# Layer 0 of a two-layer scan network: next steps projected into the sums' banks, fewer states weighed by GpSimd, output projection between the next image's spreads

## The reference, cut to what matters

```python
x_dbl = einsum('bkdl,kcd->bkcl', xs, x_proj_weight)      # per order k: 12 step columns, 16 B, 16 C
dts = einsum('bkrl,kdr->bkdl', dts, dt_projs_weight)     # the step projection
delta = softplus(dts + dt_projs_bias)                    # the steps
h = exp(delta * A) * h + (delta * u) * B                 # the scan, for each state n
y = sum over n of (h * C_n)                              # weighing, and the sum over states
```

## Time and profile before

| | |
|---|---|
| time, median of 3 | 15351.56 us (15350.93 to 15354.0) |
| profiled execution, its own time | 15355.73 us |
| its span, first to last instruction | 15353.9 us |
| mean granted TensorE clock | 0.898 of full speed |

### The profile page before, as it was taken

One profiled execution on the slowest core, in us unless ns is written; L12 is line 12 of the kernel. 1 busy time (PEld: TensorE's weight loads), 2 busy tenths in 40 slices (PEclk: granted clock), 3 DMA queues, 4 the chain that ended last, 5 costly groups with the idle time before them and its releaser, 6 DMA issues.

```text
span 15353.9 us, 137291 instructions
## 1 busy us (share of the span) xinstructions
PE 11962.6 (78%) x45056; PEld 6538.9 (43%) x45056; DVE 13974.8 (91%) x8019; ACT 10343.2 (67%) x14003; POOL 13679.9 (89%) x5828
## 2 busy tenths in 40 slices
PE   6777877778777787777877778777787777877778
PEld 4543345433444334443345433444334443345433
DVE  8998989989899899998999989999898998989988
ACT  5666766667666676666766667666676666766667
POOL 7997989979899798997889978899789997899978
PEclk8898988989889898898988989889898898988989
DMA  5662256622566225662256622666226662266622
GB/s 188 213 214 95 88 188 215 213 93 85 193 214 215 90 82 196 215 215 86 82 201 213 216 85 80 204 215 214 84 77 209 215 214 81 77 212 214 213 76 76
DMA packets 687758, 2440.08 MB, mean 159 GB/s; under 512 B 78268, under 2 KB 100040, under 8 KB 687048
## 3 DMA queue, kind: packets, MB, share of 16 engines
q1 hardware_dynamic: 687048, 2431.29, 46.6%
HBM read 2415.26 MB, written 15.73 MB: 158 GB/s over the span
## 4 chain that ended last, share of the span: by engine, by line
POOL 48%; issue 18%; DMA 11%; DVE 10%; PE 10%; ACT 3%; POOLq 0%; DVEq 0%; SPq 0%; ACTq 0%
POOL room L1186 26%; DMA room<-bc_rows 11%; POOL room L1229 7%; POOL room L1195 4%; POOL room L1232 4%; POOL room L1221 4%; DVE room L1420 4%; PE bank L720 3%; POOL room L1176 2%; PE bank L454 2%; DVE room L1355 2%; DVE u L1312 1%; DVE room L1440 1%; DVE room L1429 1%; PE bank L792 1%
## 5 line engine op out<-in xcount | busy, mean ns | idle before, releaser
L1355 DVE TENSOR_TENSOR_SCAN room<-bank,room 128x1024 f32<-128x1024 f32 x3072 | 6903.6, 2275 | 327.5 <-issue 170.2
L1186 POOL TENSOR_TENSOR room<-room 128x1024 f32<-128x1024 f32 x3072 | 7168.0, 2374 | 0.6
L930 ACT ACTIVATE bank<-room,a 128x1024 f32<-128x1024 f32 x3072 | 3429.7, 1127 | 1046.0 <-DVE room L1355 1031.7
L720 PE MATMUL bank<-room,identity 128*128 128x512 f32 x6144 | 3007.4, 640 | 855.5 <-DVE room L1440 733.2
L1420 DVE TENSOR_TENSOR_SCAN room<-bank,room 128x1024 f32<-128x1024 f32 x1536 | 3430.9, 2273 | 54.1 <-POOL room L1229 32.4
L632 PE MATMUL bank<-identity,room 128*128 128x128 f32 x19456 | 2818.1, 295 | 4.3 <-DVE room L1363 4.1
L632 PEld LDWEIGHTS bank<-identity,room 128*128 128x128 f32 x19456 | 2525.1, 154 | 524.6 <-issue 315.6
L1363 DVE TENSOR_TENSOR room<-room,bank 128x1024 f32<-128x1024 f32 x1728 | 2071.7, 1199 | 406.1 <-PE bank L584 403.0
L720 PEld LDWEIGHTS bank<-room,identity 128*128 128x128 f32 x6144 | 1200.5, 203 | 2663.4 <-issue 1270.3
L1229 POOL TENSOR_TENSOR room<-room 128x1024 f32<-128x1024 f32 x768 | 2225.5, 2921 | 56.2 <-ACT room L1051 26.7
L584 PE MATMUL bank<-parts,pick_row 96*128 96x512 bf16 x3456 | 1245.9, 421 | 718.2 <-DVE room L1363 451.4
(11 more groups left out here) (133 smaller groups left out, 11560.2 us busy)
## 6 DMA issues: line engine op xcount, KB each, us to landing
room<-bc_rows SPq DMA_DIRECT2D x4544, 512.0 KB, 4.6
wx<-in_w_x SPq DMA_DIRECT2D x65, 162.0 KB
bc_rows<-xdbl SPq DMA_DIRECT2D x72, 128.0 KB, 4.7
pictures<-in_x SPq DMA_DIRECT2D x8, 768.0 KB, 9.0
out_x<-pictures SPq DMA_DIRECT2D x8, 768.0 KB, 7.7
weights<-in_w_in SPq DMA_DIRECT2D x16, 288.0 KB, 6.7
room<-in_w_in SPq DMA_DIRECT2D x16, 288.0 KB, 5.8
room<-in_w_out SPq DMA_DIRECT2D x16, 288.0 KB, 6.2
```

The source lines that it names most:

```text
L720: ins = nc.tensor.matmul(dst, identity[:, :], rhs, start=(q == 0), stop=(q == Q - 1))
L930: nc.scalar.activation(whole(DECAY0[g % 2]), delta0[:, j, :], ACT.Exp, scale=a0[:, col:col + 1]).then_inc(S["decay"], note("decay", (i, j, ...
L1186: nc.gpsimd.tensor_tensor(source0[:, g % SOURCES, :], du0[:, (i * J + j) % 2, :], b_ring0[:, g % BROWS, :], ALU.mult).then_inc(S["source"] ...
L1355: nc.vector.tensor_tensor_scan(run(state0[:, g % STATES, :]), run(whole(DECAY0[g % 2])), run(source0[:, g % SOURCES, :]), 0.0, ALU.mult, A ...
```

## The change

Three things are changed together. The projection of the steps two passes ahead leaves the WORK banks and goes into YACC, after the old sums have been copied out and before the new ones begin (`dt_ahead`); for that the sums of n = 12 to 15 are issued in the iterations 0 and 1 instead of 0 to 2, and ScalarE's `collect` moves from its iteration n = 4 to n = 2; it copies the steps out in iteration n = 5. The units n = 2 and n = 6 that the projection no longer holds are weighed by VectorE or turned: GpSimd weighs 7 instead of 10 of the 48 units of an order (besides the units of turning back). And the output projection of layer 1 moves from one block ahead of the next image's spreads to the iterations 0, 1, 3 and 4 of that image, with semaphores of its own (mm1, ev1) and a buffer of its own; its residuals go to VectorE's iterations 5 and 9.

```diff
-SUMS0 = {0: (4,), 1: (4, 3), 2: (3,), 3: (), 4: (), 5: (5, 4)}
-LAST_SUM, FIRST_TERM = 2, 4
+SUMS0 = {0: (4, 3), 1: (3, 2), 2: (), 3: (), 4: (), 5: (5, 4)}
+LAST_SUM, NEXT_STEPS, FIRST_TERM = 1, 3, 4
+OUT1 = {0: (0, (0, 1)), 1: (0, (2,)), 3: (1, (0, 1)), 4: (1, (2,))}
 def by_pool(i, j, n):
-    return n in ((2, 6, 10, 12) if j == 0 else (2, 6, 10)) or n == 8 and turned_back(i, j) is not None
+    if n == 2:
+        return j == 1 or i * J + j == 0
+    if n == 6:
+        return j != 1 or i == K - 1
+    return n == 10 or n == 12 and j == 0 or n == 8 and turned_back(i, j) is not None
 def by_turn(i, j, n):
-    return n in ((4, 8, 14) if j == 0 else (4, 8, 12, 14)) and not by_pool(i, j, n)
+    return n in ((4, 8, 14), (4, 6, 8, 12, 14), (4, 8, 12, 14))[j] and not by_pool(i, j, n)
 def piece(g):
-    if n == (6 if j == 1 else 2) and ahead < PASSES:
-        return "dt", ahead // J, ahead % J
+    if g == 2:
+        return "dt", 0, 2
# TensorE
+            def dt_ahead(b, pass_):
+                i, j = pass_ // J, pass_ % J
+                pe.wait_ge(S[ev(last_xd(0, i))], at(ev(last_xd(0, i)), last_xd(0, i), b))
+                pe.wait_ge(S["y_turned"], at("y_turned", pass_ - 3, b))
+                for h in range(2):
+                    step = ("dt", 0, i, j) if h else ("dt_half", i, j)
+                    nc.tensor.matmul(bank[:, YACC + h, :], wdt[XR:XR + R, i % 2, j * P:(j + 1) * P],
+                                     xdbl[XR:XR + R, halves(h)], start=True, stop=True).then_inc(
+                        S["mm"], note("mm", step))
             def begin_sums(b, i, j):
                 if i * J + j > 0:
                     pe.wait_ge(S["y_turned"], at("y_turned", i * J + j - 1, b))
+                    ahead = i * J + j + 2
+                    if ahead < PASSES:
+                        step = ("dt", 0, ahead // J, ahead % J)
+                        pe.wait_ge(S["ev"], at("ev", step, b))
                 elif b > 0:
-                    pe.wait_ge(S["ev"], at("ev", ("out", 1, 0), b - 1))
+                    pe.wait_ge(S["ev1"], at("ev1", ("out", 1, 1), b - 1))
# TensorE, scans0
-                    if n == FIRST_TERM:
+                    if n == NEXT_STEPS and J <= i * J + j + 2 < PASSES:
+                        dt_ahead(b, i * J + j + 2)
+                    if b > 0 and g in OUT1:
+                        out1(b - 1, *OUT1[g])
+                    if n == FIRST_TERM and i * J + j > 0 or g == FIRST_TERM + 1:
                         begin_sums(b, i, j)
+            def out1(b, c, tiles):
+                if c == 1 and 0 in tiles:
+                    pe.wait_ge(S["ev1"], at("ev1", ("out", 1, 0), b))
+                pe.wait_ge(S["load_wout1"], at("load_wout1", 0, b))
+                for j in tiles:
+                    pe.wait_ge(S["gat"], at("gat", (1, j), b))
+                    for h in range(2):
+                        ins = nc.tensor.matmul(bank[0:CH, YACC + h, :], wout[1][:, j, c * CH:(c + 1) * CH],
+                                               y[:, j, halves(h)], start=(j == 0), stop=(j == J - 1))
+                if J - 1 in tiles:
+                    ins.then_inc(S["mm1"], note("mm1", ("out", 1, c)))
# ScalarE, scans0
-                    if g in (1, 2) and b > 0:
-                        take_out1(b - 1, g - 1)
+                    if g in (4, 6) and b > 0:
+                        take_out1(b - 1, int(g == 6))
-                    if g < len(UNITS) and n == FIRST_TERM and i * J + j > 0:
+                    if g < len(UNITS) and n == LAST_SUM + 1 and i * J + j > 0:
                         collect(b, i * J + j - 1)
+                    ahead = i * J + j + 2
+                    if g < len(UNITS) and n == NEXT_STEPS + 2 and J <= ahead < PASSES:
+                        take_dt_by_halves(b, ahead // J, ahead % J, YACC)
# VectorE
-                if g == 4 and b > 0:
-                    dve.wait_ge(S["res"], at("res", (1, 1), b - 1))
-                    if g == 3 and b > 0:
-                        residual(b - 1, 1, 0)
-                        residual(b - 1, 1, 1)
+                    if g in (5, 9) and b > 0:
+                        residual(b - 1, 1, int(g == 9))
# SyncE
-                            sp.wait_ge(S["mm"], at("mm", ("out", 1, 1), b - 1))
+                            sp.wait_ge(S["mm1"], at("mm1", ("out", 1, 1), b - 1))
```

More of the change, by code:

```diff
@@ L103, in piece @@
     i, j, n = UNITS[g]
-    ahead = i * J + j + 2
-    if n == (6 if j == 1 else 2) and ahead < PASSES:
-        return "dt", ahead // J, ahead % J
+    if g == 2:
+        return "dt", 0, 2
     if i < K - 1 and (j, n) in QUARTERS:
@@ L155 @@
     (name, 0, h) for name in ("rest", "last") for h in range(2)}
+LATE = {("out", 1, 0), ("out", 1, 1)}
 def mm(step):
-    return "mm0" if step in AHEAD else "mm"
+    return "mm0" if step in AHEAD else "mm1" if step in LATE else "mm"
 def ev(step):
-    return "ev0" if step in AHEAD else "ev"
+    return "ev0" if step in AHEAD else "ev1" if step in LATE else "ev"
 class Counts:
@@ L267, in program @@
         rs = [room[:, 13, :], room[:, 22, :]]
-        o2 = room[0:CH, 18:20, :]
+        o2 = [room[0:CH, 18:20, :], room[0:CH, 7:9, :]]
         bank = ctx.enter_context(nc.psum_tensor("bank", [P, 8, HT], F32))
@@ L282, in program @@
                  "b_line0", "b_line1", "b_line2", "c_line0", "c_line1",
-                 "xz", "shift", "silu", "mm", "ev", "mm0", "ev0", "stat0", "stat1", "gs0", "gs1", "xn", "pad", "conv", "u",
+                 "xz", "shift", "silu", "mm", "ev", "mm0", "ev0", "mm1", "ev1", "stat0", "stat1", "gs0", "gs1", "xn", "pad", "conv", "u",
                  "p1", "p2", "parts", "dl", "du",
@@ L784, in tail1 @@
                     head0(b + 1)
[L785 to L795, removed]
+                else:
+                    for c in range(2):
+                        out1(b, c, range(J))
             pe.wait_ge(loaded, 16 * LOADS)
@@ L904, in take_dt, with take_dt_by_halves @@
                     S[ev(step)], note(ev(step), step))
-            def take_dt_by_halves(b, i, j):
+            def take_dt_by_halves(b, i, j, lo):
                 for h in range(2):
-                    take(b, ("dt", 0, i, j) if h else ("dt_half", i, j), delta0[:, j, halves(h)], h)
+                    take(b, ("dt", 0, i, j) if h else ("dt_half", i, j), delta0[:, j, halves(h)], h,
+                         src=bank[:, lo + h, :])
             def softplus(b, i, j):
@@ L995, in scans0 @@
                     elif p:
-                        take_dt_by_halves(b, p[1], p[2])
-                    if g < len(UNITS) and n == FIRST_TERM and i * J + j > 0:
+                        take_dt_by_halves(b, p[1], p[2], WORK[0])
+                    if g < len(UNITS) and n == LAST_SUM + 1 and i * J + j > 0:
                         collect(b, i * J + j - 1)
+                    ahead = i * J + j + 2
+                    if g < len(UNITS) and n == NEXT_STEPS + 2 and J <= ahead < PASSES:
+                        take_dt_by_halves(b, ahead // J, ahead % J, YACC)
                     if 0 <= g - 2 < len(UNITS) and by_turn(*UNITS[g - 2]):
@@ L1091, in take_pair @@
             def take_pair(b, step, dst, banks, rows=P, func=ACT.Copy, **kw):
-                act.wait_ge(S["mm"], at("mm", step, b))
+                act.wait_ge(S[mm(step)], at(mm(step), step, b))
                 nc.scalar.activation(dst, bank[0:rows, banks[0]:banks[1] + 1, :].rearrange("p h t -> p (h t)"),
-                                     func, **kw).then_inc(S["ev"], note("ev", step))
+                                     func, **kw).then_inc(S[ev(step)], note(ev(step), step))
             def take_gate(b, j):
@@ L1115, in take_out1 @@
             def take_out1(b, c):
-                take_pair(b, ("out", 1, c), o2[:, c, :], ((YACC, YACC + 1), WORK)[c], rows=CH)
+                take_pair(b, ("out", 1, c), o2[1][:, c, :], (YACC, YACC + 1), rows=CH)
             def tail0(b):
@@ L1123, in tail0 @@
                 for c, banks in ((0, WORK), (1, SPARE)):
-                    take_pair(b, ("out", 0, c), o2[:, c, :], banks, rows=CH)
+                    take_pair(b, ("out", 0, c), o2[0][:, c, :], banks, rows=CH)
             def tail1(b):
@@ L1493, in residual @@
             def residual(b, l, c):
-                dve.wait_ge(S["ev"], at("ev", ("out", l, c), b))
-                nc.vector.tensor_tensor(xT(b)[:, c, :], xT(b)[:, c, :], o2[:, c, :], ALU.add).then_inc(
+                step = ("out", l, c)
+                dve.wait_ge(S[ev(step)], at(ev(step), step, b))
+                nc.vector.tensor_tensor(xT(b)[:, c, :], xT(b)[:, c, :], o2[l][:, c, :], ALU.add).then_inc(
                     S["res"], note("res", (l, c)))
```

## The result

The changed kernel takes 16720.28 us (median of 4 runs, 16709.92 to 16725.4) where the kernel before takes 15351.9: 1369 us more, a ratio of 1.089 (95% interval 1.0877 to 1.0903). The forecast was 16528, in a range of 16070 to 16950. The profiled execution has a span of 16721.5 us.

A forecast was written before the change was run, and what follows sets the result against it. GpSimd was taken to set layer 0's pace, with VectorE the bound after the change; terms summed to 146 us an image, 1176 us over eight images, giving 16528 us, 7.7% slower, in a range of 16070 to 16950.

The forecast's parts named there:

- 15 weighings for VectorE: VectorE weighs 231 instead of 216 states an image, at 1.11 us each: +16.7 us an image.
- the stall at 23 borders: VectorE waits for decay(3) at 22 pass borders, and 2.4 us in the last pass: +149 us an image.
- TensorE late after the pause: Step products run slow behind each stall and delay scan(6), 0.7 us a border: +15 us an image (0 to 40).
- waits for GpSimd: VectorE's waits for GpSimd in layer 0 vanish as GpSimd is relieved: -20.6 us an image.
- small decay waits: VectorE's 5.8 us of decay waits at the old collect go: -6 us an image (0 to -20).
- The pass border: Collect ahead of softplus in ScalarE's queue waits for sum 15, delaying decay(3): VectorE stands 6.2 us, 8.2 at five borders.
- The steps in YACC: Step products between collect and the next sums may run slow, delaying decay(6) and scan(6): 15 us an image (0 to 40).
- The output projection: Moved from ahead of the first spread, it halves VectorE's 16.2 us wait: -8 us an image; SyncE's waits cost nothing.
- Seven more turns: Turned states are 87 instead of 80 an image, on TensorE and ScalarE, which have room: costed at nothing.
- the relief wins: Rival: no stall at pass borders, VectorE bounds, -18 us an image, 15210 us; chance 0.04.
- TensorE staying slow: Rival: everything behind each stall runs at 1.2 GHz, 4.5 us a border, 84 us an image, 17200 us; chance 0.07.
- A dearer table switch: Rival: each ScalarE table switch costs 1.4 us more, 61 us an image, 17020 us; chance 0.03.

The follow-up runs named there:

- Run 1: Changed kernel with ScalarE's collect one iteration later, in iteration 3 behind decay(3): 15497.13 us, 1.0103 of before.
- run 2: Changed kernel with softplus ahead of collect, both still in ScalarE's iteration 2: 16302.31 us, 1.0627 of before.
- run 3: Changed kernel with softplus replaced by a relu of the same bias, so no table switch: 16215.48 us, 1.0572 of before.
- Run 5: Changed kernel with eight unread TensorE products into YACC ahead of the step products, filling the pause: 16434.21 us, 1.071 of before.
- run 10: Changed kernel with collect in iteration 3 and SyncE's store and weight load later, GpSimd still weighing 7 of 48: 15385.69 us, 1.0025 of before.
- Run 6: Changed kernel with SyncE's store and a weight load moved behind more rows in its queue: 16603.9 us, 1.0821 of before.
- run 4: Kernel before with only the output projection moved between the next image's spreads: 15343.7 us, 1.0 of before.
- Run 9: As run 8, but the middle pass's unit 6 is turned in all orders but the last, GpSimd weighing 9 of 48: 15280.39 us, 0.9955 of before.
- run 8: Changed kernel with collect in iteration 3, SyncE's two steps later, and GpSimd weighing 10 of 48 again: 15277.19 us, 0.9955 of before.
- run 7: Run 4 with the store of the image before moved behind the row of unit 18 instead of 12: 15316.33 us, 0.9982 of before.

## Why the prediction was right, and where its terms were off

The sign and the mechanism held. In us an image, second image, after less before:

| Term of the sum | Forecast | Measured | From |
|---|---|---|---|
| 15 weighings for VectorE | +16.7 | +17.4 | busy 276.3 against 258.9, one record short |
| the stall at 23 borders | +149 | +143.7 | 141.54 + 2.12 |
| TensorE late after the pause | +15 | +33.5 | 14 waits of 1.03, spreads +17.5, sums +1.6 |
| waits for GpSimd | -20.6 | -11.1 | 5.5 + 4.0 (11.9 less the 7.9 ahead of the first scan) |
| start of the image | -8 | -8.3 | 7.9 against 16.2 |
| small decay waits | -6 | -5.8 | gone |
| sum | +146 | +169 | |

(The spreads: 62.7 less 7.9 at the start, against 53.5 less 16.2. The sums: 4.6 against 3.0.) Seven images at 169.4 and a first one without the gain at the start, some 178, make 1364 of the 1369 us.

*The pass border.* The stall was to be 6.2 us and is 6.00 at 14 borders, 6.54 to 7.77 at eight. In the 3.5 us ahead of the stall the granted clock is 1.00 at those 14 and 0.56 to 0.97 at the eight: slower sums, as allowed for, though at eight borders instead of five and by less. Run 1 shows that the collect's place makes it, run 2 that the order in ScalarE's queue does, run 3 that the loads are part of it.

*The steps in YACC* is the first term that was mis-sized: 15 us an image for TensorE's late restart, against 33.5. The part that it worked out came true, 14 waits of 1.03 us for decay(6), 14.4 us. What it left out stands behind the products: the spreads (+17.5) and sums (+1.6) are late too, as turn and spread are slow with the clock at 0.50. Both ends of the range were named, 0 to 40 us an image, and the value was taken near the wrong one. Run 5 measures the whole as 36 us an image; not all of the 33.5 in the table need be the pause's, since run 10, with no stall, also waits 487.4 us for spreads where before it was 403.0.

*The output projection* is the second. "I cost that at nothing" was said of SyncE, with four rows in the ring as cover. The cover did not last: the store waits for a residual that now stands behind unit 9, the rows stand behind the store, and the GpSimd wait of 13.2 us at the start reaches VectorE as 1.74 + 2.32 + 1.33. The weight loads that wait for the moved step product, which I had not listed at all, cost GpSimd 8.6 to 9.4 us each, five times an image; before, they waited 39.2 us an image in place of 101.9, and no source stood for a row. Run 6 prices the queue at 116 us, 14.5 an image: about what is missing in the GpSimd term (9.5) and a little more. The gain at the start came (-8.3); in run 4, where GpSimd is the bound, as much was lost again through SyncE.

*Seven more turns*, costed at nothing, were not measured by themselves. Run 9 has these seven more than run 8 and seven weighings less for GpSimd, and ran as fast; but VectorE waits 102 us more for spreads in it. Whether this comes from the turns, or from VectorE being less held up by GpSimd and so there earlier, is not shown.

*The rivals.* That the relief wins is refuted twice: the stall was there, and without it (run 1, and run 10 with SyncE mended as well) the kernel is still slower than before, by 1.0 and 0.25%. TensorE staying slow was half true: the clock was 0.50 behind every stall of the second image, but that cost 36 us an image and not 84. A dearer table switch was not seen: the stall has no room for it, and run 3 gives 2.87 us a border for two loads, where that rival has 5.4.

What stays open is what makes VectorE wait for spreads at the start of an image in run 7, and how the 33.5 us divide between the slow restart and the seven more turns.

## What to carry to other kernels

An instruction moved forward in an engine's in-order queue brings its wait with it, and everything behind it pays: before moving it, find when its producer is done and what stands behind it, on this engine and on the DMA queue that waits for its result. Relief of the busiest engine is worth no more than its lead over the next one; here 56 weighings taken from GpSimd alone (run 9) changed nothing, and 15 an image handed to VectorE (run 10) cost nearly their full length. When a stall pauses TensorE, add the slow restart to its price.

## What the runs showed of the hardware

The restart is dearer than I took it to be: a pause of 8.81 us, then a clock of 0.50 in three windows of 4 us with work in each, and step products at 3.78 us; with the pause filled, 1.00 and 1.98. The Trainium skill, "TensorE: Matmul & The Clock Gate", section "HAM oscillation — how this bites in real kernels", says that a burst behind a pause starts cold each time; the trace agrees (0.50 behind the pause, at this border and at the 21 others of the image).

A switch of table on ScalarE costs its load of 1.28 us and a little more, 1.42 in all at this border: without a load the activations overlap by 0.10 us, with one they don't (run 3). The softplus starts 0.02 us behind the load, and the time without the two loads gives 2.87 us for both. The Trainium skill, "ScalarE: Activation LUTs", section "What ACT_TABLE_LOAD costs", adds a drain of about 1.38 us to each, 5.3 us for two; here trace and time are against it.
